# The x3 sum of an attention phase moved to GpSimd behind a ScalarE copy, with queries prepared two tiles ahead

## The reference, cut to what matters

```python
x = x + L0(x)   # a 32x32 matrix per batch, mixes tokens
x = x + L1(x)   # attention over a paged cache: q, k, v, rms norm, rope,
                # window of 128 positions, softmax, output projection Wo
x = x + L2(x)   # x @ W_base.T + low-rank adapter of rank 16, one of 4, chosen per batch
x = x + L3(x)   # a 32x32 matrix per batch, one of 8, mixes tokens
```

## Time and profile before

| | us |
|---|---|
| median of three runs | 279.79 (279.28 to 281.51) |
| the profiled execution | 279.48 |
| its span, first to last instruction | 277.1 |
| mean granted TensorE clock | 0.924 of full speed |

### The profile page before, as it was taken

One profiled execution on the slowest core, in us unless ns is written; L12 is line 12 of the kernel. 1 busy time (PEld: TensorE's weight loads), 2 busy tenths in 40 slices (PEclk: granted clock), 3 DMA queues, 4 the chain that ended last, 5 costly groups with the idle time before them and its releaser, 6 DMA issues.

```text
span 277.1 us, 7621 instructions
## 1 busy us (share of the span) xinstructions
PE 203.3 (73%) x2402; PEld 153.5 (55%) x2402; DVE 218.1 (79%) x631; ACT 138.0 (50%) x507; POOL 123.4 (45%) x151
## 2 busy tenths in 40 slices
PE   0050869699998999300478989989898999989773
PEld 0030756365655555100467777877777778777551
DVE  0887955889999999990458898999889889998730
ACT  0221012525555456341076787776777876677510
POOL 4366765417665555676702443444344433400000
PEclk9999966979999999955579999999999999999997
DMA  5917999104551110101412433444543334410010
GB/s 135 311 37 161 215 307 283 47 12 131 168 169 54 53 36 18 38 34 51 140 37 81 108 83 126 125 131 140 157 132 106 101 122 130 142 46 24 24 59 21
DMA packets 18863, 29.77 MB, mean 107 GB/s; under 512 B 8734, under 2 KB 14185, under 8 KB 18451
## 3 DMA queue, kind: packets, MB, share of 16 engines
q0 software_dynamic: 7408, 19.04, 25.0%
q1 hardware_dynamic: 8674, 5.29, 6.6%
q10 hardware_dynamic: 2752, 5.08, 5.8%
HBM read 29.46 MB, written 7.38 MB: 133 GB/s over the span
## 4 chain that ended last, share of the span: by engine, by line
PE 32%; ACT 7%; issue 7%; DVE 6%; DMA 2%; POOL 1%; DVEq 0%; POOLq 0%; ACTq 0%
PE bank L1138 10%; PE quad L1152 7%; PE bank L1178 4%; ACT work L664 4%; PE bank L1134 3%; PE bank L1190 3%; ACT big L647 2%; PE bank L1166 2%; PE bank L1171 2%; DVE work L967 2%; DMA big<-merged,idx 2%; DVE onT L974 1%; DVE nmx L960 1%; PE bank L1185 1%; DMA merged<-work,row_now 1%
## 5 line engine op out<-in xcount | busy, mean ns | idle before, releaser
L664 ACT ACTIVATE work<-bank,nmx 128x164 f32<-128x164 f32 x128 | 49.8, 405 | 8.4 <-DVE nmx L960 8.0
L1138 PE MATMUL bank<-kt_rope,big 128*128 128x164 f32 x256 | 46.5, 318 | 0.0
L1138 PEld LDWEIGHTS bank<-kt_rope,big 128*128 128x128 f32 x256 | 42.6, 202 | 4.2
L1134 PE MATMUL bank<-mask,identb 128*128 (+2 forms) x48 | 17.5, 364 | 33.5 <-DVE kt_rope L948 21.7
L960 DVE TENSOR_REDUCE nmx<-bank 128x3 f32<-128x492 f32 (+1 forms) x48 | 28.4, 592 | 10.6 <-PE bank L1138 10.6
L967 DVE STREAM_TRANSPOSE work<-work 128x768 f32<-128x768 f32 (+2 forms) x96 | 34.6, 408 | 0.0
L1100 PE MATMUL quad<-wqkv_sb,work 128*128 128x512 f32 x64 | 33.6, 651 | 0.0
L974 DVE TENSOR_TENSOR onT<-quad,rT 32x256 f32<-32x256 f32 x64 | 26.9, 420 | 7.3 <-PE quad L1152 5.6
L534 POOL DMA_INDIRECT big<-merged,idx x16 | 15.9, 993 | 36.8 <-DMA big<-in_pool,idx 35.6
L484 POOL DMA_INDIRECT big<-in_pool,idx x16 | 16.5, 1033 | 26.1 <-PE quad L1152 22.9
L647 ACT ACTIVATE big<-qT,con 128x256 f32<-128x256 f32 (+1 forms) x64 | 27.5, 530 | 0.1
(11 more groups left out here) (154 smaller groups left out, 445.5 us busy)
## 6 DMA issues: line engine op xcount, KB each, us to landing
merged<-big ACTq DMA_DIRECT2D x3, 1024.0 KB, 9.9
xin<-in_x SPq DMA_DIRECT2D x16, 128.0 KB, 2.8
out<-x4s SPq DMA_DIRECT2D x16, 128.0 KB, 1.8
w3bd<-w_scratch SPq DMA_DIRECT2D x64, 4.0 KB
con<-in_consts SPq DMA_DIRECT2D x1, 660.5 KB, 5.0
wqkv_sb<-in_wqkv ACTq DMA_DIRECT2D x1, 512.0 KB, 6.1
wt_sb<-in_wt ACTq DMA_DIRECT2D x1, 256.0 KB, 6.9
wp_sb<-in_wp ACTq DMA_DIRECT2D x1, 256.0 KB, 7.2
```

The lines of the kernel that those rows point to most:

```text
L664: act.activation(prob[:, p, hd, 0:NK], ps_sc[(p + i) % 2][:, j * NK:j * NK + NK], ACT.Exp, bias=nmx[:, p, hd:hd + 1], scale=1.0, accum_out ...
L1134: pe.matmul(at[:, 0:n * NK], identb[:, :], mask[:, bass.ds(t, 1), :].broadcast_to([128, n, NK]), start=True, stop=False, skip_group_check= ...
L1138: mm = pe.matmul(at[:, j * NK:j * NK + NK], qbd[:, p, hd, :], kT[:, p, hd // GSZ, 0:NK], start=False, stop=(j == n - 1), skip_group_check= ...
```

## The change

- ScalarE: `queries` is called for tile t + 2 instead of t + 1, and after the third group of exponentials instead of before it. A new copy `l2s` brings l2 of t2 from PSUM to SBUF between the second and the third group. It waits for `l2_done` and for the x3 of the tile before.
- VectorE: `scaled` does all four groups before the third maxima. The sum x3 is taken out.
- GpSimd: behind `zm` it waits for `l2s_done` and for `l3_done` and makes x3 = yall + l2s, ahead of the wait for `pv_done` and the gathers.
- TensorE: L1178 waits in addition for `l2s_done` of the tile before, since it overwrites l2 in PSUM.

```diff
@@ gpsimd, behind zm
+                    wait(l2s_done, t + 1)
+                    if reused(t):
+                        wait(l3_done, t - 1)
+                    pl.tensor_tensor(x3s[:, t % 2, :], yall[:, t, :], l2s[:, :], ALU.add).then_inc(x3_done, 1)
                 t = s - 1
                 if valid(t) and valid(t + RING):
                     wait(pv_done, t + 1)
@@ scalar, phase2
                 if valid(t):
                     exponents(1)
-                tn, _, pn, _, _ = at_step4(h, u, -1)
-                if valid(tn) and reused(tn):
+                if valid(t2):
+                    act.wait_ge(l2_done, t2 + 1)
+                    if not isinstance(t2, int) or t2 >= 1:
+                        act.wait_ge(x3_done, t2)
+                    act.copy(l2s[:, :], ps_l2).then_inc(l2s_done, 1)
+                if valid(t):
+                    exponents(2)
+                tn, _, pn, _, _ = at_step4(h, u, -2)
+                if valid(tn):
                     queries(tn, pn)
-                if valid(t):
-                    exponents(2)
@@ vector, phase2
-                    scaled(t1, range(0, 2))
+                    scaled(t1, range(G))
                 if valid(t):
                     maxima(t, p, 2)
-                if valid(t1):
-                    scaled(t1, range(2, 4))
-                if valid(t2):
-                    ve.wait_ge(l2_done, t2 + 1)
-                    if reused(t2):
-                        ve.wait_ge(l3_done, t2 - 1)
-                    ve.tensor_tensor(x3s[:, p2, :], yall[:, bass.ds(t2, 1), :].rearrange("p o n -> p (o n)"),
-                                     ps_l2, ALU.add).then_inc(x3_done, 1)
@@ tensor, phase2
                     if valid(t3):
                         pe.wait_ge(x4_done, t3 + 1)
+                        pe.wait_ge(l2s_done, t3 + 1)
```

More of the change, by code:

```diff
@@ L236, in build @@
         zm = sb("zm", [128, 128])
+        l2s = sb("l2s", [128, D])
         x3s = sb("x3s", [128, 2, D])
@@ L352, in build @@
         z_done, zs_done, zm_done, l2_done, x3_done = sem("z_done"), sem("zs_done"), sem("zm_done"), sem("l2_done"), sem("x3_done")
+        l2s_done = sem("l2s_done")
         l3_done, x4_done = sem("l3_done"), sem("x4_done")
@@ L657, in phase2 @@
                 t1, _, _, _, _ = at_step4(h, u, 1)
+                t2, _, _, _, _ = at_step4(h, u, 2)
                 t3, k3, p3, _, _ = at_step4(h, u, 3)
@@ L690, in phase2 @@
                     exponents(1)
-                tn, _, pn, _, _ = at_step4(h, u, -1)
-                if valid(tn) and reused(tn):
-                    queries(tn, pn)
+                if valid(t2):
[3 more added lines that the diff above has]
+                    act.copy(l2s[:, :], ps_l2).then_inc(l2s_done, 1)
                 if valid(t):
                     exponents(2)
+                tn, _, pn, _, _ = at_step4(h, u, -2)
+                if valid(tn):
+                    queries(tn, pn)
             steps(act, phase2, *P2R)
```

## The result

| | kernel before | changed kernel |
|---|---|---|
| median of 4 runs each | 280.01 us (279.28 to 281.51) | 289.25 us (288.27 to 291.14) |
| ratio to before, 95% interval | | 1.0333 [1.0288, 1.0378] |
| profiled execution (span) | 279.48 us (277.1) | 288.92 us (287.1) |

The change makes the kernel 3.3% slower. 291.5 us was predicted: right in sign and in mechanism, 2.6 us too much against the profiled execution.

A forecast was written before the change was run, and what follows sets the result against it. GpSimd's serial loop was taken to set the step, 9.11 us for 7.90 over 11 rounds: 279.48 + 13.3 - 2.0 + 0.85 = 291.6, given as 291.5 us; range 285.5 to 299.5.

The forecast's parts named there:

- The bound: Attention phase: after the change a serial loop through GpSimd sets the step, 9.11 us in place of 7.90.
- The string: GpSimd's loop from `zm` through L1190, l2s, x3, gathers and transfer to the next `zm`: 9.11 us, 11 rounds.
- `zm` start to x3 start: GpSimd's `zm` and 0.10 to L1190 0.51, L1190 on TensorE 0.70, ScalarE's copy l2s 0.40, 0.07 before x3.
- x3 on GpSimd: The sum x3 of two 128x256 operands on GpSimd takes 0.80 us, bounds 0.54 and 1.01.
- gap ahead of the cache gather: GpSimd's gap between x3 and the cache gather L484: 0.31 us, bounds 0.31 and 0.79.
- cache gather to merged gather: GpSimd, start of L484 to start of L534, with L529 and the 2.97 us transfer wait: 5.31 us.
- merged gather to next `zm`: GpSimd's merged gather L534 at 0.99 us and 0.02 to the next `zm`: 1.01 us.
- Rival 1: Gather lands some 1.2 us sooner, only the loop through ScalarE counts: step 8.11 us, 280.6 us; chance 0.08.
- The loop through ScalarE: Third maximum, exponentials, queries, x4s, L1178, weighted sum, all four L974, third maximum: 8.11 us, below the string's 9.11.
- The tail: After the last gathers: about two and a half steps at 7.1 us, -2.0; last x3 alone on the path, +0.85.
- Rival 3: Slower by more: gap 0.79 and sum x3 1.01 make the GpSimd loop 9.80 us, time 299.2 us; chance 0.10.

The follow-up runs named there:

- x3_part_alone: Kernel before with only the x3 part (copy l2s, sum on GpSimd behind `zm`), queries and outputs left as before: 297.84 us, ratio 1.044.
- x3_in_wait: Changed kernel with GpSimd's x3 moved between the own-block gather's issue and the wait for the cache transfer: 288.13 us, ratio 1.0092.
- x3_between: Changed kernel with GpSimd's x3 moved between the issues of the cache gather and the own-block gather: 286.32 us, ratio 1.003.
- merge_later_after: Changed kernel with the merged gather issued one step later, behind x3 and the next weighted sum: 282.35 us, ratio 1.0093.
- x3_twice: Changed kernel with GpSimd's sum made once more, into a spare buffer, just ahead of x3: 298.69 us, ratio 1.0447.
- x3_on_vector: Changed kernel with x3 on VectorE again, straight from PSUM, without the copy l2s: 285.05 us, ratio 0.9978.
- merge_later: Merged gather issued one step later: in the changed kernel, ratio 1.0093; in the kernel before, 0.9888; in the changed kernel with four query buffers, 0.9907.
- after_again: Changed kernel without any edit, run again on chip Y: 296.48 us, ratio 1.0386.

## Why the prediction came out as it did

**The bound.** Right. The wait of L1134 for the queries went, as forecast, and its 0.8 us were not gained, since the next two loops are both longer than 7.9.

**The string, term by term.** Predicted against the first measurement's trace:

| term | predicted | measured |
|---|---|---|
| `zm` start to x3 start (`zm`, L1190, copy l2s) | 1.68 | 218.17 - 216.52 = 1.65 |
| x3 on GpSimd | 0.80 | 0.73 |
| gap ahead of the cache gather | 0.31 (0.31 to 0.79) | 219.04 - 218.17 - 0.73 = 0.14 |
| cache gather to merged gather | 5.31 | 1.03 + 0.30 + 1.02 + 34.8 / 12 = 5.25 |
| merged gather to next `zm` | 1.01 | 1.01 |
| sum | 9.11 | 8.78, and 96.83 / 11 = 8.80 by the spacing |

Every step of the mechanism holds: the table has it in the trace, and that x3 on this string is what costs is shown by x3_part_alone, x3_in_wait and x3_between. The one mis-sized term is the gap: it lies outside the bounds that I gave. I took the gap of an indirect issue behind another indirect issue, 0.31, for the least that is possible. Behind an arithmetic instruction of GpSimd it is 0.14. The trace of the kernel before had one such pair, ahead of the attention phase, and I did not look for it:

```profile
26.60 1.04 POOL L465 TENSOR_TENSOR wbase_sb<-wbase_sb,con 128x128 f32<-128x128 f32 x2
27.80 1.12 POOL L440 DMA_INDIRECT w0c<-in_w,w_i  x1 [0.16 <-issue]
```

With its 0.16 the forecast would have been 8.96 a step and 290.0 us. The gap, the 0.07 of the sum and the 0.06 of the transfer make 0.3 a step, and 11 x 0.31 = 3.4 us is the overshoot of this term (100.2 forecast, 96.8 measured; 9.95 more than before in place of 13.3).

**The transfer.** Rival 1 had a quicker landing, by which the step would have been 8.1. The wait stayed at 2.90 us against 2.97, so it fell. From issue to landing L486 takes 4.3 to 5.1 us in this trace, 4.4 in the middle case. The Trainium skill's page "DMA: Bandwidth & Descriptors", section "Anatomy of one DMA", has a fixed part of about 2.0 us and the bytes at 436 GB/s, which makes an estimate of 3.2 us for the 512 KB of L486; this trace does not agree with it either.

**The sum on GpSimd.** 0.73 us for what VectorE did in 0.42, 1.7 times as long; the 0.80 that I took, next to the half-way value of two rows, was 0.07 too much.

**The loop through ScalarE.** Forecast 8.11 and no bound. In merge_later_after, where nothing longer hides it, it is 8.07. In the first measurement it was no bound, though near: TensorE waits 0.38 us for x4s in the step shown. That this loop binds the same kernel on chip Y comes from the stretched sum, which no step of mine had. The trace of the kernel before had it, small: five of its sums, those in which L534 begins, take 1.51 to 1.68 us and the others 1.41.

**The tail.** Forecast -2.0 + 0.85 = -1.15; from `zm` of tile 11 to the end of the span it was 277.1 - 241.44 = 35.66 us before and 287.1 - 251.56 = 35.54 after, -0.12. Up to the last weighted sum the gain came (-1.73 for -2.0). From there to the end of x4s it took 9.06 us in place of 9.66 (-0.60), though the end of L1190 to that of x4s in it took 2.38 in place of 1.62 (+0.76 for +0.85). Two things were not foreseen. First, windows over the last stretches, before and then after (columns as in the earlier trace rows):

```profile
264.00:270.00 6.00, 4.30 (x106) 3.14 (x87) 2.38 (x6) 0.53 (x2) 0.39 (x1) 0.91 0.20 67
270.00:277.00 7.00, 2.42 (x7) 1.11 (x5) 0.42 (x1) 0.37 (x1) 0.00 (x0) 0.74 0.07 22
```
```profile
275.00:281.00 6.00, 3.41 (x14) 2.10 (x14) 0.79 (x3) 0.99 (x3) 1.67 (x3) 1.00 0.19 66
```

Before, TensorE was granted 0.91 and 0.74 (a mixture of its two levels, 1.2 and 2.4 GHz) at the end, after, 1.00 in the stretch shown; L1178 of the last tile took 2.05 us then and 1.13 now, which more than pays for x3. Second, the end behind x4s grew from 3.76 to 5.97 us, +2.2. It is not the transfer of the last output. Its line's view from 273 us on before (L410), and from 281 us on after (L412):

```profile
DMA to landing us min/median/max: 3.3/3.3/3.3
```
```profile
DMA to landing us min/median/max: 1.7/1.7/1.7
```

It is issued at 273.37 and 281.15 and lands 3.3 us later before, 1.7 after. So the span goes on for 0.4 us behind the last landing before, and for 4.2 after. What fills these stays open: no experiment aimed at it. The tail missed its forecast by 1.0 us only because that rise and the faster clock pull against each other, which is luck.

**Sum.** 279.48 + 9.95 - 0.12 = 289.31 against 288.92 measured. That it comes so near is arithmetic on the same two traces. The rest is `zm` of tile 0, 0.17 later, and the time outside the span, 1.82 in place of 2.38 us: -0.39. Rival 3 did not come either: its far bounds of gap and sum were not met, and the clock stayed at 1.00.

## What to carry to other kernels

Before work is moved to the idlest engine, follow that engine's instructions in program order around one step: if the time between them is one serial string with a transfer in it, the engine has no room, whatever its busy share says, and each instruction put on the string costs its whole length in every round, unless another loop has become the longer one by then (x3_twice on chip Y: 0.20 of 0.73). Look at both ends of a moved instruction: hidden in its own engine's wait (x3_in_wait) it may come too late for its reader. And when a wait for a transfer is what holds an engine, try first to issue that step's dependent gather one round later: here that one move brought the changed kernel from 3.3% above the kernel before to 0.9% above it (read across two chips), and gave about 1% in the kernel before.

## What the hardware showed that was not expected

- **A gather issue in the middle of the weighted sum.** On chip Y the sum's 1.41 us of weight loads grew by 0.6 to 1.4 us when GpSimd's indirect issue (0.99 us) began inside them, and still by 0.2 to 0.7 us when it began up to 0.7 us ahead of them (x3_on_vector, x3_between). On X and Z it was 0.1 to 0.4 us, and nothing when the issue began ahead. On Y it came and went with the issue within one kernel: in x3_part_alone 9 of the 12 sums from 153 to 257 us take 2.0 to 2.8 us, and the 3 in which no issue begins, or one only 1.3 us after their start, take 1.41. On Z it was gone in the three merge_later kernels. Issues that fall into the scores' matmuls do no such harm: in after_again, with L486 and L531 in them, the matmuls of three heads take 1.00 us each time. One sum doesn't fit: in x3_part_alone the one at 271.18 takes 2.78 us, with a gap of 1.20 us, at a granted clock of 1.00 and with no GpSimd instruction near. What in the machine stops the loads, and why the price differs by chip, isn't shown. That the kernel before took 285 on Y and 280 on X and Z would go with it, but it was not profiled on Y.
- **The gap ahead of an indirect issue** on GpSimd: 0.14 us behind an arithmetic instruction, 0.30 behind another indirect issue, 0.79 where it waits for a semaphore of GpSimd's own arithmetic. In x3_between it was 0.16 behind x3.
